# Attention with a mixture of experts on one core: the routing steps dealt over four head quads, the token rows scattered over nine of them, and each batch of value products of the last quad sent some half units later

## What is computed

```python
xn = _layernorm(x, axis=-1)
# attention: Q, K, V = projections of xn, 64 (sequence, head) pairs
S = jnp.einsum('hid,hjd->hij', K, Q) * SCALE
decay = jnp.where(delta < 0, 0.0, -delta.astype(jnp.float32) ** ALPHA)
S = jnp.where(delta < 0, -jnp.inf, S) + decay
attn = jnp.einsum('hij,hjd->hid', jax.nn.softmax(S, axis=-1), V)
# experts: top 2 of 8 per token
gate_score, gate_idx = jax.lax.top_k(probs, TOP_K)
combine = jnp.einsum('tk,tke->te', gate_score, onehot) * alpha[None, :]
h = jax.nn.gelu(jnp.einsum('th,ehi->eti', x, fc1_w) + fc1_b[:, None, :], approximate=False)
y = jnp.einsum('eti,eih->eth', h, fc2_w) + fc2_b[:, None, :]
x = x + s * g          # g = silu of the experts' output
```

## Time and profile before

| | |
|---|---|
| runs | 722.7 us median of 3 (719.65 to 725.21) |
| the profiled execution | 723.35 us, span of its instructions 721.5 us |
| PE | 682.4 us busy (95%) |
| DVE | 535.4 us busy (74%) |
| ACT | 485.1 us busy (67%) |
| POOL | 231.4 us busy (32%) |
| DVE L1103, 608 reductions of pieces | 357.9 us, 653 ns each |
| ACT L967, 576 exponentials | 304.0 us, 603 ns each |
| PE L1578, value products | 154.9 us, 498 ns each (1536 records) |
| PE's granted clock, mean | 0.981 |
| chain that ended last | PE 82%, DVE 8%, DMA 6% |

### The profile page before, as it was taken

The page is one execution under the profiler, slowest core; times in us unless marked ns, Lnnn a source line. Parts: engine busy times, 40 slices in busy tenths (PEclk is TensorE's granted clock), DMA queues, the critical chain, the costliest instruction groups (busy, mean ns, idle before and its releaser), DMA issues.

```text
span 721.5 us, 17539 instructions
## 1 busy us (share of the span) xinstructions
PE 682.4 (95%) x6042; PEld 462.0 (64%) x6042; DVE 535.4 (74%) x1146; ACT 485.1 (67%) x994; POOL 231.4 (32%) x330
## 2 busy tenths in 40 slices
PE   6976999999999999999999999999789999999976
PEld 3865776565555556556555655654359888999764
DVE  6535987999989989998998999896224554444298
ACT  3542443677777877788787777878776666666374
POOL 5331110134023323423342432300034757576300
PEclk9997999899999999999999999999999999999998
DMA  6999966333765685487568657710359686865396
GB/s 194 267 251 308 350 215 198 96 57 74 127 128 138 140 178 148 120 173 159 137 139 171 142 141 149 169 25 19 94 132 251 244 206 216 223 189 177 112 401 245
DMA packets 77207, 124.46 MB, mean 172 GB/s; under 512 B 14184, under 2 KB 47464, under 8 KB 77000
## 3 DMA queue, kind: packets, MB, share of 16 engines
q1 hardware_dynamic: 68368, 98.32, 54.4%
q0 software_dynamic: 8752, 25.02, 10.8%
HBM read 72.56 MB, written 49.72 MB: 169 GB/s over the span
## 4 chain that ended last, share of the span: by engine, by line
PE 82%; DVE 8%; DMA 6%; ACT 2%; issue 2%; POOL 1%; SPq 0%; DVEq 0%; POOLq 0%; ACTq 0%
PE ps L1578 20%; PE ps L1511 14%; PE ps L1562 13%; PE ps L1667 8%; PE ps L1689 8%; PE ps L1500 7%; PE ps L1460 5%; PE ps L1470 3%; DMA arena<-in_x 2%; DMA arena<-xs_dram 2%; PE ps L1650 2%; DVE mxa L1103 2%; DVE arena L1412 1%; DVE x_room L1417 1%; DVE arena L1402 1%
## 5 line engine op out<-in xcount | busy, mean ns | idle before, releaser
L1103 DVE TENSOR_REDUCE mxa<-ps 128x1 f32<-128x512 f32 (+3 forms) x608 | 357.9, 653 | 35.2 <-PE ps L1500 20.3
L967 ACT ACTIVATE arena<-ps 128x512 f32<-128x512 f32 x576 | 304.0, 603 | 82.3 <-PE ps L1562 41.1
L1511 PE MATMUL ps<-aug 57*128 57x512 f32 (+3 forms) x768 | 218.4, 401 | 2.1 <-DVE mxa L1103 0.3
L1562 PE MATMUL ps<-aug 59*128 59x512 f32 (+3 forms) x768 | 216.0, 399 | 0.5 <-ACT arena L967 0.5
L1578 PE MATMUL ps<-arena,v_q 128*32 128x512 f32 (+3 forms) x1536 | 154.9, 498 | 6.7 <-ACT arena L967 6.3
L1562 PEld LDWEIGHTS ps<-aug 59*128 59x128 f32 x768 | 109.9, 186 | 76.2 <-ACT arena L967 69.0
L1511 PEld LDWEIGHTS ps<-aug 57*128 57x128 f32 x768 | 109.6, 186 | 37.2 <-DVE mxa L1103 23.4
L889 POOL DMA_INDIRECT y_dram<-arena,y_row_of x71 | 69.4, 978 | 54.2 <-DVE y_row_of L1341 47.3
L862 POOL DMA_INDIRECT xs_dram<-arena,slot x64 | 62.6, 978 | 74.1 <-ACT arena L967 70.5
L1500 PE MATMUL ps<-key_mask,key_rows 64*128 64x64 bf16 (+2 forms) x704 | 79.0, 208 | 0.0
L1667 PE MATMUL ps<-arena 128*128 128x128 f32 x568 | 75.2, 275 | 0.0
(11 more groups left out here) (148 smaller groups left out, 639.3 us busy)
## 6 DMA issues: line engine op xcount, KB each, us to landing
aug<-k_parts SPq DMA_DIRECT2D x96, 128.0 KB
aug<-q_parts SPq DMA_DIRECT2D x96, 128.0 KB
arena<-xs_dram SPq DMA_DIRECT2D x71, 128.5 KB, 2.6
k_parts<-arena SPq DMA_DIRECT2D x16, 512.0 KB, 5.9
q_parts<-arena SPq DMA_DIRECT2D x16, 512.0 KB, 5.9
arena<-y_dram SPq DMA_DIRECT2D x16, 512.0 KB, 6.7
xn_dram<-arena SPq DMA_DIRECT2D x8, 512.0 KB, 6.9
a_dram<-arena SPq DMA_DIRECT2D x128, 32.0 KB
```

The costliest lines, as they stand in the source:

```text
L967: nc.scalar.activation(prob_slot(q, i), score_bank(q, i), ACT.Exp).then_inc(exp_done, 1)
L1103: nc.vector.tensor_reduce(dst, src, AX.X, ALU.max).then_inc(piece_used, 1)
L1511: ins = nc.tensor.matmul(banks[:, at_ * width:(at_ + 1) * width], k_aug[n][rows, hp, ib * P:(ib + 1) * P], q_aug[n][rows, hp, lo:lo + widt ...
L1562: ins = nc.tensor.matmul(out_[:, col0:col0 + hi - lo], q_aug[n][rows, h // SIDES_OF_ARRAY, jb * P:(jb + 1) * P], k_aug[n][rows, h // SIDES ...
```

## The change

Four tables or numbers move, and the code follows them.

- `LAST_BATCH_AFTER` from (6, 11, 15, 19, 23, 27, 31, 35) to (7, 13, 18, 22, 26, 30, 33, 35).
- The steps: `choose_experts` goes over quads 0 (from item 3, each fourth) and 1 (each fourth), `place_bases` to quad 2 (each third), `place_tiles` to quad 3 (each third). `counts` goes to item 20 of quad 1 (`COUNTS_IN` = 1), and with it ACT's small exponential (L974).
- `MOVE_FROM` from 2 to 4: the 32 tiles are scattered in nine quads (4 to 12) by 3, 4, 3, 4, 3, 4, 3, 4, 4, where it was 2 and ten times 3. The place of a fourth tile is added to `BETWEEN_BATCHES`. Pads are cleared in quads 5 to 12.
- The first load of biases (window 3) goes; window 6 loads both parts. POOL copies the values for quads 1 and 2 ahead of the wait for the counts, and the waits for weights count one load less.

```diff
@@
-LAST_BATCH_AFTER = (6, 11, 15, 19, 23, 27, 31, NU - 1)
+LAST_BATCH_AFTER = (7, 13, 18, 22, 26, 30, 33, NU - 1)
@@
-BETWEEN_BATCHES = ((25, 27, 29), (NU + 5, NU + 6, NU + 8))
+BETWEEN_BATCHES = ((23, 25, 27, 29), (NU + 3, NU + 5, NU + 6, NU + 8))
@@
+COUNTS_IN = 1
@@
-MOVE_FROM = 2
+MOVE_FROM = 4
@@
-    return PRO + WIN * q + (q > 0)
+    return PRO + WIN * q + (q > COUNTS_IN)
@@
-    return items[:COUNTS_AT] + [("counts", 0, 0)] + items[COUNTS_AT:] if q == 0 else items
+    return items[:COUNTS_AT] + [("counts", 0, 0)] + items[COUNTS_AT:] if q == COUNTS_IN else items
@@
-                else:
+                elif t > 0:
                     sp.wait_ge(routed, 1)
                     sp.wait_ge(pads_ready, 1)
+                    experts = slice(per * t if t > 1 else 0, per * (t + 1))
                     for dst, src in ((b1_sb, b1), (b2_sb, b2)):
-                        sp.dma_start(dst[:, per * t:per * (t + 1), :],
-                                     src[:, per * t:per * (t + 1), :]).then_inc(moe_w_in, 16)
+                        sp.dma_start(dst[:, experts, :], src[:, experts, :]).then_inc(moe_w_in, 16)
@@
+            next_v(0, 0)
+            next_v(1, 1)
             pool.wait_ge(counts_out, 1)
@@
-            next_v(0, 0)
+            next_v(2, 2 % AUG)
             pool.wait_ge(shares_ready, 1)
@@
-            next_v(1, 1)
+            next_v(3, 3 % AUG)
@@
-                    if i == SHARES_STEP and first:
+                    if i == SHARES_STEP and q == COUNTS_IN:
@@
-            follow(0, choose_experts(), ROUTE_FROM)
-            follow(1, place_bases(), every=2)
-            follow(2, place_tiles(), every=2)
-            for q in range(3, NQ - 1):
+            choosing = choose_experts()
+            follow(0, choosing, ROUTE_FROM, every=4)
+            follow(1, choosing, every=4)
+            follow(2, place_bases(), every=3)
+            follow(3, place_tiles(), every=3)
+            for q in range(4, NQ - 1):
                 follow(q)
```

More of the change, by code:

```diff
@@ L995, in take_weights @@
                 nc.scalar.activation(w1_now[j % 2], w1_sb[:, bass.ds(e * KT, KT), :], ACT.Copy).then_inc(w1_ready, 1)
-            act.wait_ge(moe_w_in, 16 * 2 * AUG * ROUNDS)
+            act.wait_ge(moe_w_in, 16 * 2 * (AUG * ROUNDS - 1))
             act.wait_ge(xgT_out, EARLY + 2)
@@ L1329, in x_evacuate_first @@
                 nc.vector.tensor_copy(xgT[n], bank(n)[:, 0:D]).then_inc(xgT_out, 1)
-            dve.wait_ge(moe_w_in, 16 * 2 * AUG * ROUNDS)
+            dve.wait_ge(moe_w_in, 16 * 2 * (AUG * ROUNDS - 1))
             dve.wait_ge(pv_done, batches_done(NQ - 1, EARLY_FREE))
@@ L1609, in window @@
                     half_unit(q, n, i)
-                    count = ITEMS_AFTER[i] + (first and i == COUNTS_STEP)
+                    count = ITEMS_AFTER[i] + (q == COUNTS_IN and i == COUNTS_STEP)
                     if i in batch_after:
@@ L1695, in _ @@
             send_batch(NQ - 1, (NQ - 1) % AUG, NB - 1)
-            pe.wait_ge(moe_w_in, 16 * 2 * AUG * ROUNDS)
+            pe.wait_ge(moe_w_in, 16 * 2 * (AUG * ROUNDS - 1))
             pe.wait_ge(routed, 1)
```

## The result

The changed kernel takes 717.6 us (median, 714.1 to 724.0), beside 724.1 us (719.3 to 728.6) for the kernel before on the same chip: a ratio of 0.9925, with a 95% interval of 0.990 to 0.995, or 5.4 us less by the ratio (the medians lie 6.5 apart). I had said 719.5 us and no change of over 1%. The experiments ran later, on three chips (which chip the first comparison had isn't recorded), and there the kernel before takes 737 to 740 us and the changed one 761; they take that up.

A forecast was written before the change was run, and what follows sets the result against it. Bounds: DVE too full in the first quads, PE and ACT waiting for each other in the last, PE between. Last quad -4.8, routing +0.6, scatter +1.0 gave -3.2 us: 720.15 profiled, 719.5 us forecast, range 715.8 to 723.5.

The forecast's parts named there:

- The last quad: Last quad: batches sent five half units behind what they need leave ACT no pause from exponential 14; gain 4.8 us.
- PE's idles, which I expected to remain: Last quad: PE's idles end earlier but remain, since PE is not the bound there.
- the rival with 0.08: First expert tiles: PE's fifth tile stands behind attention loads, giving back the last quad's gain; 724.3 us, chance 0.08.
- The queue should be empty by then: Behind the attention: argument against the rival with 0.08, that the DMA queue is empty when the fifth tile is loaded.
- The routing: Quads 0 to 3: spread steps cost 6.55 us over steady quads against 6.0 before, so 0.6 us more.
- the claim that PE's delay and DVE's lie beside each other: Quad 0: low-clock PE delay and DVE's step delay, 3.1 us each, overlap; only the longer is paid.
- DVE would pause again ahead of items 6 and 14: Quad 0: sign that DVE's slack returns, with steps at items 3, 7 and 11 free.
- the end of the prologue: Quad 0: 1.2 of the 5.5 us over a steady quad, counted as staying.
- the clock stays up, or falls for half as long: Quad 0: rival in which the low clock stretch vanishes or halves, 2.7 us better; 716.8 us, chance 0.24.
- three further meetings of POOL's copy with DVE: Quads with scatters: later landings make POOL's copy meet DVE three more times, about 0.3 us each; 1.0 us more.
- the sign that I had named: Quads with scatters: DVE L1109 (L1112 after) takes over 0.3 us in more quads than now.
- The rival on the slow side: Quads 5 to 13: scatter landings meet DVE in most, 0.5 to 0.65 us a quad; 724.4 us, chance 0.12.

The follow-up runs named there:

- e4: Kernel before with the last quad's batches sent one half unit later instead of up to four; 733.7 us in one execution, last quad 21.3 us.
- e10_spaced_again: Kernel before with the new last-quad table and indirect DMAs behind half units 24, 28, 32 (0, 4, 8 of the next quad), second run; 724.2 us, ratio 0.984.
- e1: Kernel before with only the new table for the last quad's batches; 734.6 us beside 738.4, ratio 0.9937.
- e11: Changed kernel with its four tiles a quad behind half units 23, 26, 29, 32 (-1, 2, 5, 8 of the next); 739.2 us, ratio 0.998.
- e9: Same kernel as e10_spaced_again, first run; 720.7, 721.9, 733.8 and 734.0 us beside 740.3 of the kernel before.
- e6: Kernel before, unchanged, run again on a later chip; 733.5 us in its one execution (the kernel before: 736.9 median).
- e5: Changed kernel, unchanged, run again on a later chip beside the kernel before; 760.7 us, ratio 1.031.

## Why the prediction was right, and where it wasn't

**The last quad: right, a little small.** I gave it 4.8 us; it is 5.4 in all nine profiles with the new table (19.0 against 24.4). The mechanism is the one told: ACT never pauses once the cover is four or five half units; with three (e4) it pauses 0.2 us. It starts earlier than I worked out, with exponential 8 and not 14, because batch 1 also comes two half units later, and an exponential takes 0.502 us (14.05 / 28) and not 0.517. PE's idles, which I expected to remain, nearly vanish (busy for 18.1 of 19.0 us).

**The fifth expert tile: the rival with 0.08 came, in part.** The waits of PE behind the attention, in after and then in e10_spaced_again (who waited for whom: us, times, longest):

```profile
PE ps L1655 <- DMA arena<-xs_dram: 1.1, 1, 1.1
```

```profile
PE ps L1650 <- DMA arena<-xs_dram: 1.8, 1, 1.8
PE ps L1667 <- ACT arena L984: 0.9, 1, 0.9
```

The kernel before has no such wait there. It is the fifth tile, as that rival named it: against the loads ahead of it PE comes to it about 5 us earlier, and its load is issued behind others that still run. PE waits there in six of the nine kernels with the new table, 1.1 to 1.8 us, and seven have a wait of 0.9 to 1.4 us for ACT 19 us behind the attention. In the first comparison the stretch behind the attention still is no longer (189.5 against 189.7), but on the later chips it is 190.8 to 192.1 us in seven of eight kernels with the new table and 188.0 to 189.5 with the old. That is some 2 us given back; e1's 4.6 us, uncertain by 2.5 either way, can't tell it from none. "The queue should be empty by then" is the step that failed: in after the eight loads of the inverse sums land from 527.7 to 533.8 us, and the fifth tile's load, issued among them at 530.7, lands at 535.3. In before that load is issued at 534.1, where the DMA share has been 0.00 for 2 us, and such loads land after 2.4 us (median) instead of 4.5.

**The routing: +0.6 us in the sum, 0.5 to 1.2 us of gain by the profiles.** No run has the spread routing alone, so this is read from quads. Fourteen profiles let me sort quad 0 by its low clock. The old placing (seven): six with 6.8 us of low clock at 30.4 to 30.7 us, one with 3.4 us at 31.7. The new placing (seven): none in four, 27.6 to 27.7 us; 3.4 us in two, 28.9; 6.8 us in one, 29.8. I had 27.75 for none (24.9 + 1.65 + 1.2) and 30.45 for the full stretch, so the sum was right, and the claim that PE's delay and DVE's lie beside each other nearly so: with the stretch still there (one profile) the spread steps bring 0.6 to 0.9 us, not the 2.1 that DVE alone would say. The parts of the sum are another matter. I had named as a sign that DVE would pause again ahead of items 6 and 14, and it doesn't. Timeline of DVE in after, around item 6 of quad 0:

```profile
129.64 0.41 DVE L1209 TENSOR_TENSOR arena<-logits,arena 128x256 f32<-128x256 f32 x1
129.97 2.48 DVE L1106 TENSOR_REDUCE mxa<-ps 128x2 f32<-128x512 f32 x4
132.36 0.42 DVE L1212 SCALAR_TENSOR_TENSOR arena<-arena,num_sb 128x256 f32<-128x256 f32 x1
```

It runs on like this, without a wait, to 150.58. So the steps at items 3, 7 and 11 were not free: nine steps of 0.33 come to 3.0 us and would alone fill the 2.75 us that quad 0 is over 24.9, with nothing left for the 1.2 that I had put down to the end of the prologue. That 27.75 was met owes something to luck.

What I had wrong besides is how often the clock falls: the rival "the clock stays up, or falls for half as long" got 0.24 and was true in six of seven. The windows view of after around its low clocks, the fall and the 3.4 us ahead of it, quads 0 and 14:

```profile
146.20:149.60 3.40, 3.40 (x29) 2.06 (x29) 3.40 (x8) 2.33 (x5) 0.00 (x0) 0.50 0.06 12
504.60:508.00 3.40, 3.40 (x24) 0.90 (x16) 0.00 (x0) 1.54 (x3) 0.00 (x0) 0.50 0.49 157
501.20:504.60 3.40, 3.40 (x26) 2.26 (x29) 0.28 (x1) 3.40 (x8) 0.00 (x0) 1.00 0.04 7
142.80:146.20 3.40, 3.38 (x35) 2.32 (x32) 3.26 (x8) 2.30 (x6) 0.00 (x0) 1.00 0.01 2
```

PE was busy for 3.38 and 3.40 of 3.40 us ahead of each, as in the earlier trace rows. The Trainium skill's rule that activity releases the throttle (TensorE: Matmul & The Clock Gate, Part 1: The HAM clock gate) doesn't say why the clock fell here, though its outcome, a quad 0 whose clock stays up when DVE holds PE up less, is what came more often. The second of these stretches costs quad 14 its 1.6 us; such a stretch is in quad 14 of three profiles, all with the new placing, and in none of the other eleven. What sets it I leave open.

Quads 1 to 3 cost more than I gave them: 27.1 (26.7 in five of the six other profiles), 25.7 and 25.5 against 26.1, 25.4 and 25.5. Quad 1 is the largest miss, 0.6 us in five profiles and 1.0 in the other two. It holds POOL's running sums now, and the maxima's operations meet them. Timeline of DVE, then of POOL, in after:

```profile
169.62 0.29 DVE L1112 TENSOR_TENSOR mxa<-mxa 128x16 f32<-128x16 f32 x1
169.95 0.27 DVE L1114 CAST msplit<-mxa 128x32 fp32r<-128x32 f32 x1
170.25 0.53 DVE L1116 TENSOR_TENSOR msplit<-mxa,msplit 128x32 fp32r<-128x32 f32 x1
```

```profile
169.22 0.66 POOL L809 TENSOR_TENSOR arena<-arena 128x224 f32<-128x224 f32 x1
...
170.13 0.60 POOL L809 TENSOR_TENSOR arena<-arena 128x192 f32<-128x192 f32 x1
```

Elsewhere these take 0.18, 0.18 and 0.19, so 0.5 us are lost here, on top of the counts. The Trainium skill (GPSIMD Engine Reference, 1. Specifications) says that POOL contends with DVE instructions in a 2-port perf mode or with two SBUF inputs; the two TENSOR_TENSOR agree (0.29 and 0.53). The CAST with its one input lost 0.09 as well; whether it ran in such a mode no run shows. I priced POOL's copy against DVE for the scatter and left POOL's sums out. They stood beside the maxima before the change too, in quad 0 (0.29, 0.18, 0.19), and the larger loss depends on how they fall: it is in the two profiles in which quad 1 takes 27.1 us (after, e11) and in quad 0 of e9, while in the five at 26.7 only 0.1 us is lost. Some 0.5 us of quad 1's miss stays open in all seven. In quad 2 the CAST beside POOL's slot sums takes 0.44 instead of 0.18 in all seven profiles with the new placing, about as much as quad 2 is over my 25.4. In sum the routing gives quad 0 an average of 28.3 instead of 30.7, and takes 1.2 to 1.9 back.

**The scatter: near in size in the first comparison, by other ways, and blind to the rest.** In the first comparison quads 4 to 12 grew by 1.5 us (I had 1.0), but not by three further meetings of POOL's copy with DVE. There are fewer: quad 12's, from which I priced them, is gone (L1112 takes 0.17 there), against the sign that I had named, and quad 10's was there before and became longer. Timeline of DVE in quad 10, before and then after:

```profile
397.39 0.33 DVE L1109 TENSOR_TENSOR mxa<-mxa 128x16 f32<-128x16 f32 x1
```

```profile
396.32 0.35 DVE L1112 TENSOR_TENSOR mxa<-mxa 128x16 f32<-128x16 f32 x1
...
396.93 0.49 DVE L1116 TENSOR_TENSOR msplit<-mxa,msplit 128x32 fp32r<-128x32 f32 x1
```

The last of these took 0.19 before. That is 0.3 of the 0.7 us by which quad 10 grew, and at the end of quad 11 PE waits 0.76 us at 432.40 for the transposed maxima's DMA, a wait that I hadn't thought of. On the later chips quads 4 to 12 grow by 34 us from e6 to e5, and the whole kernel is 24 us slower than the one before. The rival on the slow side ended there, but by none of the mechanisms that I gave it: the 0.47 us a quad from which it decides was passed eight times over (34 / 9 = 3.8) by late starts of ACT and DVE beside back-to-back indirect DMAs, and by the low clock that came with them. Slower by over 1% was a case to which I gave 0.04. The trace of before could not show it, since there the same three in a row stand beside ACT's exponentials without a mark. The size is known, the cause on the chip isn't; nor why the first comparison was free of it.

**The sum.** From the two profiles: the start -1.2, quad 0 -1.5, quads 1 to 3 +1.8, quads 4 to 13 +1.45, quad 14 +1.55, quad 15 -5.4, behind -0.2, together -3.5 of the 3.6 us of span, where I had -3.2. The start's -1.2 stands in no term of mine, nor does quad 14's +1.55. That the profiled forecast (720.15 against 719.89) came so close is luck in part: a low clock in quad 14 took back the gain of quad 0. Over all executions the ratio puts the change at 5.4 us there.

## What to carry to other kernels

A batch that waits for its newest input wants as much work of the other engine behind it as the batch and the first item after it take; count that cover in time, and shift the whole table until the pause in the timeline is gone. Then look at what the earlier start meets: the next stage's loads were queued for the old time. Beside engines that hand work to each other about every half microsecond, try indirect DMAs at other places and further apart: sent mostly 1.7 to 3.0 us apart instead of 1.28, and at other half units, the same transfers cost 3.4 us over ten quads instead of 11.1 in the measurements that showed the disturbance. And time a change of a few per cent again, later and on a second chip, before it is believed.

## What was not expected of the hardware

- One program, two kinds of outcome: the changed kernel takes 717.6 us in one comparison and 760.7 in another, the kernel before 724.1 and 736.9 to 740.3. Nearly all of the difference stands in quads with indirect DMAs (25.0 against 26.0 us with three tiles, 25.0 against 28.6 to 30.8 with four at the changed kernel's places); quads 14 and 15 without a low clock agree within 0.1 us for the same table.
- In the later measurements, and not in the first, indirect DMAs issued 1.28 us apart go with starts of ACT and DVE 2 us and more (2.4 in the rows shown) behind products that PE's records show as done, while POOL keeps its pace and PE goes on until it lacks their results.
- In quads held up like this the low clock appears as well (0.89 and 0.94 in quads 4 and 5 of e5), so that a stall costs more than its own length.
